# Adding the layer norm's two halves on VectorE before the mean and variance matmuls, with all queues of the layer loop reordered

## What is computed

```python
for i in range(DEPTH):   # 6
    x = attn_layer(shift_tokens(x), Wqkv[i], q_scale[i], k_scale[i], Wo[i]) + x
    x = ffn_layer(shift_tokens(x), ln_g[i], ln_b[i], W1[i], b1[i], W2[i], b2[i]) + x

def ffn_layer(x, g, bln, W1, b1, W2, b2):
    mu = x.mean(-1, keepdims=True)
    var = ((x - mu) ** 2).mean(-1, keepdims=True)
    xn = (x - mu) / jnp.sqrt(var + 1e-05) * g + bln
    a, gate = jnp.split(xn @ W1 + b1, 2, -1)
    return a * jax.nn.gelu(gate, approximate=False) @ W2 + b2
```

## Time and profile before

| | |
|---|---|
| time, median of 3 runs | 3271.23 us (3268.61 to 3271.33) |
| span of the profiled execution | 3280.4 us |
| TensorE busy | 3087.2 us, 94%, 29936 matmul pieces |
| VectorE busy | 2638.4 us, 80% |
| ScalarE busy | 2534.1 us, 77% |
| GpSimd busy | 2084.0 us, 64% |

### The profile page before, as it was taken

The page is one execution under the profiler, slowest core; times in us unless marked ns, Lnnn a source line. Parts: engine busy times, 40 slices in busy tenths (PEclk is TensorE's granted clock), DMA queues, the critical chain, the costliest instruction groups (busy, mean ns, idle before and its releaser), DMA issues. The chain is left out here.

```text
span 3280.4 us, 80720 instructions
## 1 busy us (share of the span) xinstructions
PE 3087.2 (94%) x29936; PEld 2736.1 (83%) x29936; DVE 2638.4 (80%) x5117; ACT 2534.1 (77%) x7059; POOL 2084.0 (64%) x1536
## 2 busy tenths in 40 slices
PE   5898886689999999999999999999999999999997
PEld 4666664479998999989999989999899998999996
DVE  3378888878789888788878898878988878888884
ACT  2787885478787888788888888888788887888784
POOL 5347655776666666666666676667676767666661
PEclk8888996799999999999999999999999999999998
DMA  3111100110001000001100011000100000110000
GB/s 128 55 36 49 59 4 7 42 36 11 2 2 34 25 26 2 2 21 33 31 2 2 11 34 39 1 2 2 37 26 22 2 1 21 33 31 7 8 5 26
DMA packets 27780, 75.04 MB, mean 23 GB/s; under 512 B 4120, under 2 KB 9848, under 8 KB 27256
## 3 DMA queue, kind: packets, MB, share of 16 engines
q1 hardware_dynamic: 22224, 52.63, 5.1%
q0 software_dynamic: 4864, 16.78, 1.6%
q10 hardware_dynamic: 304, 0.47, 0.1%
HBM read 65.68 MB, written 4.19 MB: 21 GB/s over the span
## 5 line engine op out<-in xcount | busy, mean ns | idle before, releaser
L1596 POOL TENSOR_TENSOR turned<-by_cos,turned 128x512 f32<-128x512 f32 x384 | 494.5, 1288 | 827.5 <-DVE turned L2101 827.0
L1600 POOL TENSOR_TENSOR rnorm<-norm,half 128x8 f32<-128x8 f32 x384 | 789.1, 2055 | 0.0
L1883 ACT ACTIVATE prob<-ps_s,ebias,rnorm 128x128 f32<-128x128 f32 x1536 | 681.8, 457 | 64.9 <-DVE ebias L2122 64.2
L2115 DVE TENSOR_REDUCE negmax<-ps_s 128x8 f32<-128x1024 f32 x192 | 235.0, 1224 | 284.0 <-PE ps_s L1698 283.9
L1892 ACT ACTIVATE prob_t<-ps_t 128x512 f32<-128x512 f32 x384 | 230.3, 600 | 223.4 <-PE ps_t L1707 218.8
L2130 DVE TENSOR_TENSOR prob<-prob,rinv 128x512 f32<-128x512 f32 x384 | 375.8, 979 | 13.1
L1642 PE MATMUL ps_qk<-w_hi,x_hi 128*128 128x512 f32 x768 | 336.8, 438 | 18.8 <-DVE turned L2101 12.2
L1787 PE MATMUL ps_f<-hid_hi,w_hi 128*128 128x256 f32 (+1 forms) x1056 | 309.3, 293 | 5.7 <-DVE hid_lo L2176 5.6
L1883 ACT ACTIVATION_READ_ACCUMULATOR prob<-ps_s,ebias,rnorm 128x1 f32 x1536 | 311.1, 203 | 0.0
L1642 PE MATMUL ps_qk<-w_lo,x_hi 128*128 128x512 f32 x768 | 305.8, 398 | 0.0
L1642 PE MATMUL ps_qk<-w_hi,x_lo 128*128 128x512 f32 x768 | 305.7, 398 | 0.0
(11 more groups left out here) (289 smaller groups left out, 9779.6 us busy)
## 6 DMA issues: line engine op xcount, KB each, us to landing
w_raw<-in_w_qkv SPq DMA_DIRECT2D x24, 768.0 KB, 4.8
w_raw<-in_w SPq DMA_DIRECT2D x12, 693.0 KB, 4.0
w_raw<-in_w_o SPq DMA_DIRECT2D x12, 512.0 KB, 3.4
w_raw<-in_w SPq DMA_DIRECT2D x6, 768.0 KB, 4.4
x_tok<-in_x SPq DMA_DIRECT2D x8, 256.0 KB, 2.7
kept<-x_t SPq DMA_DIRECT2D x8, 256.0 KB, 2.0
w_raw<-kept SPq DMA_DIRECT2D x8, 256.0 KB, 3.1
out<-rows_out SPq DMA_DIRECT2D x8, 256.0 KB, 2.2
```

The source lines that it names most:

```text
L1596: G.tensor_tensor(turned[:, k, :], by_cos[:, :], turned[:, k, :], ALU.add).then_inc(s["turned"], 1)
L1600: G.tensor_tensor(rnorm[:, i % RR, :], norm2[:, k, :], half[:, :], ALU.pow).then_inc(s["rnorm"], 1)
L1883: last = A.activation(prob[:, k, h, :], half_bank(h % 2, k)[:, T(h // 2)], ACT.Exp, bias=ebias[:, i // NU % 2, k, h:h + 1], scale=rnorm[:, ...
L2115: V.tensor_reduce(negmax[:, k, :, :].rearrange("p u (c o) -> p o u c", o=2), ps_s[:, :, :].rearrange("p o (u c k) -> p o u c k", u=NU, c=2 ...
```

## The change

Two sums move from TensorE to VectorE. `add_x` is followed by an addition of the two tiles of x1 into `halves`, so `mean_mm` is one matmul instead of two. ScalarE's squares are followed by `add_squares`, which adds their two tiles into `squares`, so `var_mm` has 2 matmuls instead of 4. The squares move to tiles 3 and 4 of `hidden` instead of tiles 0 and 1 of `gate`, and with them the waits of `square`. `w_2_mm(q, 0)` is cut into the tiles 0 to 2, a step earlier, and 3 to 5. The queues are put in a new order; for the helpers that repeat:

On ScalarE `hidden_hi(1)` moves from phase 1 to phase 7, right behind `hidden_hi(0)`; `square` of phase 1 moves ahead of `project`; `hidden_read(0)` moves behind `attend`. On GpSimd `hidden_lo(1)` of phase 3 stands ahead of `rotated` instead of behind it. The core of the diff:

```diff
-    cent, cent_sq = hidden[:, 0:KT, :], gate[:, 0:KT, :]
+    cent, cent_sq = hidden[:, 0:KT, :], hidden[:, 3:3 + KT, :]
+    halves, squares = hidden[:, KT, :], gate[:, KT, :]
...
         def mean_mm(q):
-            E.wait_ge(s["lx1"], q + 1)
+            E.wait_ge(s["x1_and_halves"], 2 * q + 2)
...
-            for kt in range(KT):
-                last = E.matmul(ps_f[1][:, 0:N], mean_w[:, :], shifted(x1[:, q % 2, :])[:, kt, :], start=kt == 0, stop=kt == KT - 1)
-            last.then_inc(s["mean"], 1)
+            E.matmul(ps_f[1][:, 0:N], mean_w[:, :], halves, start=True, stop=True).then_inc(s["mean"], 1)
...
         def var_mm(q):
-            E.wait_ge(s["cent2"], q + 1)
+            E.wait_ge(s["cent_and_squares"], 2 * q + 2)
             for u in range(NU):
-                for kt in range(KT):
-                    last = E.matmul(ps_f[1][:, N + u:N + u + 1], cent_sq[:, kt, T(u)], mean_w[:, 0:1], start=kt == 0,
-                                    stop=kt == KT - 1)
+                last = E.matmul(ps_f[1][:, N + u:N + u + 1], squares[:, T(u)], mean_w[:, 0:1], start=True, stop=True)
...
-        def w_2_mm(q, mt):
+        def w_2_mm(q, mt, tiles):
...
-            for j in range(NJ):
+            for j in tiles:
...
         def square(q):
-            A.wait_ge(s["cent"], q + 1)
+            A.wait_ge(s["cent_and_squares"], 2 * q + 1)
             if q:
-                A.wait_ge(s["hid_lo"], 2 * q)
+                A.wait_ge(s["gated"], 2 * q)
...
         def add_x(q):
             V.wait_ge(s["w_o"], NU * (q + 1))
             V.tensor_tensor(whole(x1[:, q % 2, :]), ps_f[0][:, :].rearrange("p (k n) -> p k n", k=KT), whole(state[:, q % B, :]),
-                            ALU.add).then_inc(s["lx1"], 1)
+                            ALU.add).then_inc(s["x1_and_halves"], 1)
+            V.wait_ge(s["x1_and_halves"], 2 * q + 1)
+            if q:
+                V.wait_ge(s["gated"], 2 * q - 1)
+            by_half = shifted(x1[:, q % 2, :])
+            V.tensor_tensor(halves, by_half[:, 0, :], by_half[:, 1, :], ALU.add).then_inc(s["x1_and_halves"], 1)
...
+        def add_squares(q):
+            V.wait_ge(s["cent2"], q + 1)
+            if q:
+                V.wait_ge(s["hid_lo"], 2 * q - 1)
+            V.tensor_tensor(squares, cent_sq[:, 0, :], cent_sq[:, 1, :], ALU.add).then_inc(s["cent_and_squares"], 1)
...
+            for q in passes(t, 24):
+                gate_value(q, 1)
...
             for q in passes(t, 0):
                 take_x(q)
...
-            for q in passes(t, 25):
-                gate_value(q, 1)
```

## The result

The changed kernel took 3315.01 us (median of 4 runs, 3308.76 to 3321.73) against 3271.28 us, a ratio of 1.0131 with the interval 1.0109 to 1.0154. Timed again in five rounds the ratio was 1.0118 (1.0102 to 1.0134). So it is some 40 us slower; I had forecast 27 us more and a range that ended at 3308 us. The direction and the main place were right, the size was not.

The account below looks back on a forecast made before the run. TensorE, busy 2456.85 of 2480 us, was taken to bound the kernel. 45 x (1.15 - 0.41 - 0.09) = +29 us, layers -2, gave +27: 3298 us, its own range 3284 to 3308, 8 in 10 range 3232 to 3308.

Parts of the forecast that it names:

- What bounds, and the mechanism: TensorE's queue bounds; in phases 7 and 0 the moved gate product puts x_hi and x_lo behind GpSimd operations, +1.15 us per pass.
- the forecast's chain: Phases 7 to 1: negmax 1.73 us later, halves 0.45 more, then weigh's product, flip_prob, and flip_qk 1.21 us late.
- Rival (1): VectorE keeps its turn, x_hi runs straight behind gate_value(1): each pass 0.65 us shorter, 3237 us, range 3226 to 3250; chance 0.22.
- Rival (2): Smaller delay, x_lo gets in before hid_lo or only flip_prob waits: 3265 to 3278 us; chance 0.06.
- Rival (3): The mean does otherwise than said; with prob_t early and both cuts counting, 3217 us; chance 0.02.
- rival (4): The halves also wait for GpSimd's L1600, flip_prob 1.5 us later still: 3365 us; chance 0.03.
- Mean: Phase 0: 0.44 us leaves TensorE's queue, but flip_qk of phase 1 waits for prob_t; gain 0.
- the first step: On the mean in phase 0: a shorter mean makes the wait for prob_t 0.71 us instead of 0.27 and brings nothing.
- Variance and order: Variance ahead of the projection of phase 2: 0.41 us less; new sequence of matmuls and flips: 0.09 us less, per pass.
- Phase 6: weigh behind the first read, ahead of w_o_mm(0): VectorE gains 0.3 us, TensorE about 0.15 us of its wait.
- Layer starts: Five passes: hid_lo waits go (-6.5 us), tables cost +3.3, weight split 0.25; together -2 us, between -6 and +4.
- The first and last passes: The first two and the last of 48 passes, beside other work or alone, left out of the 45 counted.

Follow-up runs that it names:

- x first: Changed kernel with one VectorE swap in phase 0: the split of x ahead of the second half of the gate product; ratio 0.9928 to the kernel before.

## Why the prediction was right and wrong

**What bounds, and the mechanism: right.** `x_lo` 2.21 us (forecast about 2.2), `x_hi` 0.83 (0.8), `negmax` 1.73 us late (1.73). From `flip_qk` of phase 0 to that of phase 1 it is 5.52 us instead of 4.28, 1.24 more (1.21). But the shares of this 1.21 were partly wrong. The delay enters TensorE at the projection of phase 0, which the forecast named only in passing; it is the main wait. With the gate product's move alone, without the halves, the same distance is already 5.43 us, 1.14 more, where the forecast's chain without its 0.45 us for the halves has 1.21 - 0.45 = 0.76. So, as far as the two kernels can be compared, the halves add 0.10 us and not 0.45, and the 1.21 came out since two errors met: luck had a part in that.

**The rivals.** Rival (1) fell: with 0.06 us between the release and its issue, `x_hi` lost its turn in every pass. Rival (2) fell with it: `x_lo` took 2.20 to 2.22 us in all of them. The run with x first comes to about what rival (1) described (3237 us, range 3226 to 3250), by another order: by its ratio it is 0.9928 x 3271.3 = 3248 us. Rival (3) fell, since the mean's cut is eaten in each kernel here; rival (4) too: the halves are not held by the power.

**Mean: 0 was about right, by a different way.** The mean's place is 0.36 us shorter in the changed kernel, because `flip_prob` is late while ScalarE's copies of v are not, and `prob_t` follows it sooner (0.69 us behind its start in the rows above, 1.00 before). But the halves make `flip_prob` wait (0.39 us in the projection's place) and the flips are slower (0.06 and 0.14 us; with the gate product's move alone these three places are as before). So it is lost again, and some 0.2 us with it. Where `flip_prob` is on time, the wait grows from 0.27 to 0.71 us, as the first step said.

**Variance and order: right.** -0.46 us against -0.50. **Phase 6:** -0.26 against -0.15, and 0.07 more at `flip_qk` of phase 7, which the sum didn't have.

**An ordinary pass** is 0.74 us longer, forecast 0.65: 0.09 x 45 = 4 us of the miss.

**Layer starts: wrong.** Forecast -2 us. In the four passes around each of the five starts the kernel before spends 12.5 us in all above an ordinary pass, the changed one 15.4: +2.9, so 4.9 us of the miss. The waits for `hid_lo` went. In their place TensorE loses 0.86 us in phase 0 (I took 0.65), 0.86 us in phase 2 behind the weight split of phase 1 (I took 0.25, with 1.5 as the bound), and 0.79 instead of 0.43 us in phase 4, a term that the sum didn't have. That the 0.86 us of phase 2 are the weight split's alone is not shown: without the squares' sum 0.21 us are left of such a loss. The other passes of the 45 give 1.8 us back, 1.1 of them in the last, so that all 45 are 34.45 us longer.

**The first and last passes: wrong.** I gave them 0, since they "run beside other work or alone". They cost 5.7 us: 3.8 up to the first mean, 1.3 to the second, 0.6 from the last but one to the end (there the engines are 1.0 us faster and the output's transfers 1.6 us slower, which may be scatter). The 3.8 come for the most part with the new order: `weigh` stands behind the other block's instructions in the first 16 steps, and TensorE waits up to 4.1 us for its product. The kernels in the old order have 111.0 to 112.5 us there. The diff showed that move, and I read the queues of the repeating helpers alone.

Together 4 + 4.9 - 1.8 + 5.7 = 13 us, which leads from +27 to the +40 measured. The range ended at +37. It had no term for the first and last passes, and it was narrower than its own terms: 0.85 us a pass and +4 at the layers make 45 x 0.85 + 4 = +42.

## What to carry to other kernels

When an instruction is moved in a queue of VectorE, lay it out against GpSimd's queue in time: the cost is not only its duration but whose turn it takes. Here two instructions of 0.42 and 0.70 us became 0.83 and 2.21 us. Before work is taken from the busiest engine, look at what ends the next wait on it; 0.44 us of matmul came back as 0.44 us of waiting, and an addition whose input came late cost 113 us. And read a new queue order in all stretches where it runs, the first steps and the layers' starts too, because a moved helper passes neighbours there that the steady pass doesn't have.

## What I had not expected of the hardware

I had not expected that the turns fall so evenly: `x_hi` was issued 0.06 us behind the release in my working, which I took for open (rival 1 had 0.22), and in the 44 passes of the changed kernel it lost its turn each time (mean 835 ns), as in the kernel with the gate product moved alone. Nor that the power waits for its turn (2.10 instead of 1.65 us) and yet lets VectorE's products through at their full speed. Nor that the part of the program ahead of the layers, the same instructions each time, ended anywhere from 577.7 to 593.1 us in the profiled executions, the later the lower its granted clock (0.87 down to 0.85), so that a difference of two spans (27.1 us here) missed the layers' own (40 us) by a third.
